# Threshold digits of a mixture-of-experts router moved into an attention loop, counted on GpSimd

## The reference

```python
energy = jnp.einsum('nhqd,nhkd->nhqk', q, k)            # 16 heads of 8, T = 1024
attn = softmax(energy / sqrt(8), axis=3)
out = jnp.einsum('nhql,nhld->nhqd', attn, v)
...
capacity = max(1, int(Sz * CAP_FACTOR / E) + 1)         # 257
scores = softmax(jnp.einsum('bsd,ed->bse', x, router_w), axis=-1)
gate_vals, sel_idx = jax.lax.top_k(swapaxes(scores, 1, 2), capacity)
# tokens = x[b_idx, sel_idx]; two-layer expert with gelu; times gate; scatter-add
```

## Time and profile before

| | us |
|---|---|
| median of 3 runs | 1981.02 (1980.35 to 1981.33) |
| the profiled execution | 1978.19 |
| its span | 1976.4 |
| mean granted TensorE clock of the span | 0.919 of full speed |
| plain attention loop, first to last maximum (L1241) | 1011.4 to 1661.1 |
| its end stretch, to the last division (L1258) | 1661.4 to 1713.0 |

### The profile page before, as it was taken

The page is one execution under the profiler, slowest core; times in us unless marked ns, Lnnn a source line. Parts: engine busy times, 40 slices in busy tenths (PEclk is TensorE's granted clock), DMA queues, the critical chain, the costliest instruction groups (busy, mean ns, idle before and its releaser), DMA issues. The chain is left out here.

```text
span 1976.4 us, 40754 instructions
## 1 busy us (share of the span) xinstructions
PE 1741.5 (88%) x15061; PEld 901.7 (46%) x15061; DVE 1399.7 (71%) x3172; ACT 1151.1 (58%) x2314; POOL 581.1 (29%) x817
## 2 busy tenths in 40 slices
PE   5699999999999968799659999999999999687895
PEld 2356666666666545476312222222232332255563
DVE  6676766767788356542569999999899998656431
ACT  3336666666656632222328898989888887432231
POOL 2312122221122146677440000003310000167774
PEclk9779999999999978879768999999999998689888
DMA  5642744454540053232230000000000000062334
GB/s 162 162 84 50 129 90 78 96 98 72 92 89 12 23 150 60 34 59 36 77 127 9 28 18 18 24 29 18 18 18 24 28 3 23 17 171 38 60 40 84
DMA packets 108005, 120.95 MB, mean 61 GB/s; under 512 B 14360, under 2 KB 72960, under 8 KB 107808
## 3 DMA queue, kind: packets, MB, share of 16 engines
q1 hardware_dynamic: 83616, 100.97, 21.7%
q0 software_dynamic: 24192, 17.38, 6.4%
HBM read 81.71 MB, written 35.65 MB: 59 GB/s over the span
## 5 line engine op out<-in xcount | busy, mean ns | idle before, releaser
L1241 DVE TENSOR_REDUCE mx<-wide 128x2 f32<-128x1024 f32 x512 | 590.8, 1218 | 44.8 <-PE wide L1154 43.4
L1275 ACT ACTIVATE pT<-bank 128x512 f32<-128x512 f32 x1024 | 556.3, 595 | 89.5 <-PE bank L1147 79.1
L903 ACT ACTIVATE pT<-bank 128x512 f32<-128x512 f32 (+3 forms) x768 | 344.0, 490 | 238.8 <-PE bank L757 229.9
L1147 PE MATMUL bank<-q_st,k_st 51*128 51x512 bf16 x1024 | 341.1, 395 | 14.9 <-ACT pT L1275 7.6
L1154 PE MATMUL wide<-k_st,q_st 48*128 48x512 bf16 x1024 | 328.8, 400 | 23.8 <-DVE mx L1241 13.9
L1163 PE MATMUL bank<-pT,vst 128*32 128x256 f32 x4096 | 338.0, 403 | 0.0
L870 DVE TENSOR_REDUCE mx<-wide 128x1 f32<-128x640 f32 (+3 forms) x256 | 256.8, 1021 | 90.6 <-PE wide L772 86.5
L757 PE MATMUL bank<-q_st,k_st 122*128 122x512 f32 (+3 forms) x768 | 297.5, 397 | 6.9 <-ACT pT L903 5.0
L764 PE MATMUL wide<-k_st,q_st 120*128 120x512 f32 (+3 forms) x768 | 270.8, 370 | 20.3 <-PEq L371 11.7
L1860 POOL DMA_INDIRECT acc_rows<-yg,idx x128 | 201.9, 1577 | 102.0 <-DVE yg L2127 66.0
L1147 PEld LDWEIGHTS bank<-q_st,k_st 51*128 51x128 bf16 x1024 | 77.3, 94 | 260.2 <-ACT pT L1275 209.2
(11 more groups left out here) (328 smaller groups left out, 2008.6 us busy)
## 6 DMA issues: line engine op xcount, KB each, us to landing
q_st<-rope_split SPq DMA_DIRECT2D x60, 256.0 KB
k_st<-rope_split SPq DMA_DIRECT2D x60, 256.0 KB
qk_split<-parts SPq DMA_DIRECT2D x8, 1024.0 KB, 6.3
q_st<-qk_split SPq DMA_DIRECT2D x96, 64.0 KB
k_st<-qk_split SPq DMA_DIRECT2D x96, 64.0 KB
qk_parts<-parts SPq DMA_DIRECT2D x8, 768.0 KB, 4.6
xn_rows<-xn SPq DMA_DIRECT2D x8, 512.0 KB, 4.0
w1b<-in_L_ffn_w SPq DMA_DIRECT2D x16, 256.0 KB, 5.2
```

Of the source, the lines that this page charges most:

```text
L903: e.activation(pT[:, u % NPB, q0:HALF], bank[place_of[u]][:, q0:HALF], ACT.Exp, scale=scale).then_inc(s_p, 1)
L1147: e.matmul(bank[place_of[u]][:, :], k_st[at][64 * r:64 * r + KROW, jj, kc * P:(kc + 1) * P], q_st[at][64 * r:64 * r + KROW, jj, J * HALF:( ...
L1241: e.tensor_reduce(mx[G % 2][:, kh, pair:GH:2, c], wide[w % 2][:, :].rearrange("p (r k) -> p r k", r=2), AX.X, ALU.max).then_inc(s_sf, 1)
L1275: e.activation(pT[:, u % NPB, :], bank[place_of[u]][:, :], ACT.Exp, scale=scale).then_inc(s_p, 1)
```

## The change

1. The early steps lie closer. The two norm steps stay in half 18. The other ten stand in halves 19 to 23, two to a half, at begin + 11 and + 14. What is lent is the bank that is idle in that half (`idle_bank`: bank 3 in even halves, 2 in odd ones). GpSimd's multiplications move to t = 304 and 306.
2. Twelve of the 15 digits stand in halves 24 to 29, two to a half. For each, VectorE makes the trials (begin + 3, or + 8), GpSimd counts the hits (in its own program at the same t), TensorE sums the counts into three columns of the idle bank (begin + 7, or + 13), VectorE reads the total (begin + 8, or + 14) and gives the bank back. TensorE waits for the count, and for the bank.
3. GpSimd's count (`pool_digits`) has no accumulator: three comparisons of 128 columns into `hits`, six folds that halve the width, and a last addition into `count`. Behind each of these it waits for its own semaphore.
4. The end stretch keeps `late_step`, and has six steps left of 18: three digits with VectorE's accumulating comparisons, and the three behind the digits.

The diff, cut. Its additions at the end of a t stand in TensorE's loop behind the turn of the maximum (`s_mt`), in VectorE's behind the division of an output (`s_y`), in GpSimd's behind the split (`s_m3`); `digit_read` stands ahead of VectorE's reduce.

```diff
-            lent = bank[3][:, :]
-            routed = Router(buf, 0, lent, lent[:, HALF - 2 * CPH * NE:HALF], results,
-                            (wide[1][:, HALF:2 * HALF], wide[0][:, HALF:2 * HALF]))
+            LENT, COUNTED = range(19, 24), range(24, 30)
+            idle_bank = lambda h: 2 + (h + 1) % 2
+            digits = [(NP * h, first) for h in COUNTED for first in (True, False)]
+            digit_tried = {begin + (3 if first else 8): i for i, (begin, first) in enumerate(digits)}
+            digit_summed = {begin + (7 if first else 13): i for i, (begin, first) in enumerate(digits)}
+            digit_read = {begin + (8 if first else 14): i for i, (begin, first) in enumerate(digits)}
+            lent = [bank[idle_bank(h)][:, :] for h in LENT]
...
-            LENT = range(9, 15)
-            step_at = [2 * NP * s + at for s in LENT for at in (11, 14)]
-            last_of = [2 * NP * s + 14 for s in LENT]
+            step_at = [18 * NP + at for at in (11, 14)] + [NP * h + at for h in LENT for at in (11, 14)]
+            last_of = [NP * h + 14 for h in LENT]
...
-                uses += [(2 * NP * s + 14, 2 * NP * s + 19, 3, ("lent", s)) for s in LENT]
+                uses += [(NP * h + 14, NP * h + 19, idle_bank(h), ("lent", h)) for h in LENT]
+                uses += [(t, t + 2, idle_bank(t // NP), ("digit", i)) for t, i in digit_summed.items()]
...
                                      identb[:, :], start=True, stop=True).then_inc(s_mt, 1)
+                        if t in digit_summed:
+                            bank_free(ahead_of["digit", digit_summed[t]])
+                            next(steps)
...
                          if t in step_at:
                             next(steps)
+                        if t in digit_read:
+                            next(steps)
+                            e.sem_inc(s_lent, 1)
...
                                              rsum[:, :, :, :].broadcast_to([P, CPH, GH, HD]), ALU.mult).then_inc(s_y, 1)
+                        if t in digit_tried:
+                            next(steps)
...
                              next(sums, None)
-                        if t in (19 * NP + 10, 19 * NP + 12):
+                        if t in (19 * NP, 19 * NP + 2):
                             next(normed)
...
                              e.tensor_tensor(part[:, :, 2, :], mxr[:, :, :], part[:, :, 1, :], ALU.subtract).then_inc(s_m3, 1)
+                        if t in digit_tried:
+                            next(counted)
...
+            def pool_digits(self, e):
+                def then(ins):
+                    self.chained += 1
+                    ins.then_inc(self.gp, 1)
+                    e.wait_ge(self.gp, self.chained)
+
+                hits = self.hits
+                for i in range(len(self.sums)):
+                    e.wait_ge(self.inv, i + 2)
+                    for j in range(3):
+                        ins = e.tensor_scalar(hits[:, j, :], self.byrow[:, :], self.trials[:, j:j + 1].bitcast(F32), None, ALU.is_ge)
+                    then(ins)
+                    width = P // 2
+                    while width > 1:
+                        then(e.tensor_tensor(hits[:, :, 0:width], hits[:, :, 0:width], hits[:, :, width:2 * width], ALU.add))
+                        width //= 2
+                    if i:
+                        e.wait_ge(self.tot, PRIME + i)
+                    e.tensor_tensor(self.count[:, :], hits[:, :, 0], hits[:, :, 1], ALU.add).then_inc(self.cnt, 1)
+                    yield
...
                 for i in range(NDIGIT):
-                    if i == 0:
+                    if i < len(self.sums):
+                        if i == 0:
+                            then(e.tensor_copy(self.trials[:, :], digit_units[:, 0, :]))
+                        else:
+                            then(e.scalar_tensor_tensor(self.trials[:, :], digit_units[:, i, :], self.taken[:, 0:1],
+                                                        self.found[:, :].broadcast_to([P, 3]), ALU.bitwise_xor, ALU.bitwise_xor))
+                            mark(e.tensor_tensor(self.found[:, :], self.found[:, :], self.taken[:, :], ALU.bitwise_xor))
+                        e.sem_inc(self.inv, 1)
+                    elif i == 0:
...
-                    e.matmul(self.totals[:, 0:3], same_row[:, :], self.count[:, :], start=True, stop=True).then_inc(self.tot, 1)
+                    e.matmul(self.total_of(i), same_row[:, :], self.count[:, :], start=True, stop=True).then_inc(self.tot, 1)
```

More of the change, by code:

```diff
@@ L1139, in bank_free @@
                             e.wait_ge(s_m, PRIME + n + 1)
+                        elif kind == "digit":
+                            e.wait_ge(s_lent, len(LENT) + n + 1)
                         else:
@@ L1173, in _ @@
                         if t - 3 in step_at:
[L1174 to L1178, removed]
+                            h, at = divmod(t - 3, NP)
+                            if h in LENT and at == 11:
+                                bank_free(ahead_of["lent", h])
                             next(steps)
@@ L1497, in __init__, with logits, total_of @@
                 self.known = sem("gates_known")
-                self.logits = counts[:, 0:CPH * NE].rearrange("p (c e) -> p c e", c=CPH)
+                self.counts = [one[:, HALF - 2 * CPH * NE:HALF] for one in sides] if sides else [counts] * 4
                 self.totals = (late[1] if late else counts)[:, CPH * NE:CPH * NE + 16]
+            def logits(self, q):
+                return self.counts[q][:, 0:CPH * NE].rearrange("p (c e) -> p c e", c=CPH)
+            def total_of(self, i):
+                return self.sums[i] if i < len(self.sums) else self.totals[:, 0:3]
             def xn_of(self, q, c):
@@ L1611, in vector @@
                     e.wait_ge(self.lg, PRIME + q + 1)
-                    then(e.tensor_copy(self.prob[:, q % 2 * CPH:(q % 2 + 1) * CPH, q // 2, :], self.logits))
+                    then(e.tensor_copy(self.prob[:, q % 2 * CPH:(q % 2 + 1) * CPH, q // 2, :], self.logits(q)))
                     yield
@@ L1628, in vector @@
                 e.wait_ge(self.t, PRIME + 1)
-                then(e.tensor_copy(self.byrow[:, :], self.side[:, 0:P]))
+                then(e.tensor_copy(self.byrow[:, :], self.sides[4][:, 0:P]))
                 yield
@@ L1647, in vector @@
                     e.wait_ge(self.tot, PRIME + i + 1)
-                    then(e.tensor_scalar(self.passes[:, :], self.totals[:, 0:3], float(CAP), None, ALU.is_ge, ALU.add,
+                    then(e.tensor_scalar(self.passes[:, :], self.total_of(i), float(CAP), None, ALU.is_ge, ALU.add,
                                          accum_out=self.digit[:, :]))
@@ L1702, in scalar @@
                     e.wait_ge(self.tr, PRIME + q + 1)
-                    e.activation(self.xnT[q % 2][:, :], self.side[:, :], ACT.Copy).then_inc(self.ev, 1)
+                    e.activation(self.xnT[q % 2][:, :], self.sides[q][:, :], ACT.Copy).then_inc(self.ev, 1)
                     yield
@@ L1722, in tensor @@
                     for c in range(CPH):
-                        ins = e.matmul(self.logits[:, c, :], self.xnT[q % 2][:, c * P:(c + 1) * P], rwt[:, :], start=True, stop=True)
+                        ins = e.matmul(self.logits(q)[:, c, :], self.xnT[q % 2][:, c * P:(c + 1) * P], rwt[:, :], start=True, stop=True)
                     ins.then_inc(self.lg, 1)
```

21 lines of the change are left out of this document (13 added, 8 removed).

## The result

The changed kernel takes 2023.20 us (median of 4, 2018.85 to 2028.04), the kernel before in the same comparison 1981.17 us (1980.35 to 1983.75): a ratio of **1.0215, 95% interval 1.0184 to 1.0245**. It is slower by 42 us; 42.6 were forecast. The profiled execution took 2026.51 us.

What follows compares the result with a forecast made beforehand. VectorE (0.9 us slack a half), TensorE and ScalarE, tied by short queues, bound the plain loop. Six halves at +8.1 us, +48.6, less 6 at the end, give +42.6 on 1981.0: 2023.6 us, range 2006 to 2044.

Steps and rivals of the forecast that it cites:

- The wait: TensorE at the product of the maximum (L1229), halves 24 to 29: empty 5.9 us each, split queued behind second count.
- mis-sized term: GpSimd's comparisons in each digit's count: 0.34 us each, three 1.0 us, within a count of 3.7 us.
- a rival with 5 us: GpSimd slower than its rows, 5 us a count: +2 us a half, 2036 us in all; chance 0.08.
- The clock: Behind each wait in halves 24 to 29: slow t's of 2.04 us, 0.8 us lost in each of 2.8, 2.2 us.
- The rival in which the clock holds: Halves 24 to 29 lose only the wait: 6 x 5.9 = 35, less 6, 2010 us; chance 0.08.
- The sum for a half: Each of halves 24 to 29: 6.1 + 2.2 less 0.2, 8.1 us longer; six halves +48.6 us.
- the last term: VectorE's digit work in halves 24 to 29: only the second digit's reading, 0.4 us, counted in the half's sum.
- the rival "not slower": Short wait at the maximum's product, leaving VectorE's 1.2 us a half: 1982 us, or 1979; chance 0.04.
- The end stretch: Last stretch, twelve of 15 digits gone: gain 6 us, between 0 and 9, near 45 us instead of 51.6.
- The first digit's count: GpSimd's first count in halves 24 to 29: done 0.9 us before TensorE wants it, so nobody waits.
- The moved steps: Five routing steps with work, moved to halves 19 to 23: still 2.15 us each, sum of the move 0.
- GpSimd and VectorE: Rival: they contend at the merge of maxima under the first count, 3.5 us over six halves, 2027 us; chance 0.08.

Runs made afterwards that it cites:

- The kernel that holds the clock: Changed kernel plus 48 matmuls whose results are overwritten, on TensorE ahead of its wait for the split in halves 24 to 29; 1987.71 us, ratio 1.0206.
- The split-first kernel: Changed kernel with GpSimd's second count queued behind the split of the maximum; 1956.68 us, ratio 1.004; run again on a third chip 1951.25 us, ratio 1.0013.
- the repeated one: Kernel before and changed kernel, both unchanged, run again on other chips: before 1955.16 us, ratio 1.0012 against itself; changed 1995.76 us, ratio 1.0216.
- the kernel with the steps alone: Kernel before with only the ten early steps moved to halves 19 to 23, all 15 digits left in the end stretch; 1957.68 us, ratio 1.0053.

## Why the prediction was right

**The wait was foreseen with its place and its size.** L1229 waits six times, for L1342, 6.1 us each on TensorE; 5.9 were predicted, and for VectorE's next reduce 5.64 where 5.7 were. Inside it two sizes were off and cancelled. The count is 4.45 us, not 3.7. The folds came out right, 2.32 us for six and 0.20 for the last addition; the comparison was the **mis-sized term**: three took 1.76 us, 0.60 each, where I had 0.34 from a copy of twice the width in 0.40 us. A comparison against a value in memory isn't priced by a copy's row, and I had kept that case for a rival with 5 us. Against that, the count started 0.60 us behind TensorE's arrival (1545.09 to 1545.69), and I had 0.9, plus 0.2 for gaps that were not there: 0.60 + 4.45 + 1.06 = 6.11.

**The clock.** Predicted 2.2 us a half, from the one wait in half 18. The kernel that holds the clock gives 2.2 to 2.3. The slow t's behind the wait are 1.98 us apart, near the 2.04 that I took; I had counted 2.8 of them, and the first half with digits has two, the next one three. The rival in which the clock holds is refuted by 0.82 to 0.88 in the traced halves.

**The sum for a half is 9.0 us, not 8.1** (172.8 us for six against 118.8). By the kernels above it is 5.4 for standing still, 2.2 for the clock and 1.4 for two digits on which nothing waits; I had 5.7, 2.2 and 0.4, less 0.2. So most of the missing 0.9 is in the last term. I had counted only part of the second digit on the path, since VectorE's slack was to hide the rest. The split-first kernel has that term alone, 1.3 to 1.4 us a half, near the 1.2 that I had used in the rival "not slower" and left out of my own sum. VectorE is busy 1.2 us longer in those halves (20.15 us against 18.93), so I take the term for VectorE's; no kernel took its digit instructions away and kept the rest, so this isn't shown.

**The end stretch** was to give 6 us, between 0 and 9, and to take near 45 us. It took 39.2 and gave 12.4 in the profiled pair, beyond my own bound, and 3.5 in the repeated one. I had assumed the first eight t at the low clock of before. ScalarE's timeline of after:

```profile
1725.52 1.57 ACT L1289 ACTIVATE pT<-bank 128x512 f32<-128x512 f32 x3 [1.52 <-PE bank L1155]
...
1740.86 9.03 ACT L1289 ACTIVATE pT<-bank 128x512 f32<-128x512 f32 x18 [0.29 <-PE bank L1155]
1751.15 0.60 ACT L1295 ACTIVATE o_sb<-bank 128x512 f32<-128x512 f32 x1 [1.27 <-PE bank L1171]
```

The clock in that window is 0.96, and the last nine t pass in 9.03 us. With 0.67 before, I take the difference to be mostly clock (no run holds the clock there), and the clock of this stretch is no fixed property: 0.67 and 0.85 in two traces of before, 0.96 and 0.79 in two of after. **So 42.6 was met by luck, because two errors cancelled**: in the traces of the first pair the loop and the end give +55.0 - 12.4 = +42.6, I had +48.6 - 6. With the second pair it is +53.9 - 3.5 = +50.4, and the rest of that kernel was 3.4 us shorter.

**The first digit's count** was to be ready 0.9 us early. With 4.45 us instead of 3.7 that margin is used up. Count, weighing and sum in the second half with digits:

```profile
1569.98 0.64 PE L1171 MATMUL bank<-pT,vst 128*32 128x256 f32 x8
...
1570.26 0.19 POOL L1618 TENSOR_TENSOR count<-hits 128x3 bf16<-128x3 f32 x1
...
1570.60 0.16 PE L1786 MATMUL bank<-count,same_row 128*128 128x3 bf16 x1
```

In all six halves the sum starts 0.34 us behind the start of the count's last instruction, so TensorE takes it as it arrives. That is 0.58 to 0.62 us behind the start of the weighing, and 0.57 to 0.58 for the second digit, whose count is long done: the wait is 0.05 us at most. The rival with a slower GpSimd, 5 us and a wait of 0.4 for the first digit too, didn't happen, but it was close.

**The moved steps** cost nothing in the loop, as predicted: 630.4 us for it in the kernel with the steps alone. The 8 us by which that kernel's median is longer are not explained.

**GpSimd and VectorE** don't get in each other's way here. GpSimd in the first half with digits, and the merge of the maxima, a VectorE instruction on SBUF, under its folds:

```profile
1539.73 2.32 POOL L1614 TENSOR_TENSOR hits<-hits 128x192 f32<-128x192 f32 x6
```

```profile
1540.83 0.18 DVE L1259 TENSOR_TENSOR mxw<-mx 128x16 f32<-128x16 f32 x1
```

In the halves without digits it took 0.17 or 0.18 us, too, and it started as soon behind the reduce ahead of it. The folds of the second count, under which no merge stands, take the same 2.32 us. The Trainium skill (SBUF — State Buffer, "Who interferes with whom") lets the second of two such instructions wait for the first; at 16 columns no trace here shows it.

**What I hadn't in the sum** is that the profiled execution of after is 48.3 us longer than that of before, not 42.6. The part ahead of the loop was 2.5 us shorter, and the second mixture, from VectorE's first reading of an expert's result from a bank to its last, took 8 us more, with the same work on every engine and a lower clock. Windows of before and of after over the same work:

```profile
1748.00:1952.00 204.00, 175.19 (x1279) 121.07 (x1278) 97.24 (x508) 60.19 (x114) 146.25 (x113) 0.92 0.36 61
```

```profile
1788.00:2000.00 212.00, 179.27 (x1281) 124.16 (x1280) 97.62 (x507) 60.22 (x114) 146.37 (x113) 0.89 0.34 59
```

In the repeated pair it is the other way round (192.9 us before, 188.5 after). The 192.9 us of that kernel before:

```profile
1730.40:1923.30 192.90, 171.15 (x1279) 121.02 (x1278) 97.29 (x507) 60.30 (x114) 146.46 (x113) 0.92 0.38 63
```

They come with the same mean clock, 0.92, as the 204.0 of the first chip, so the clock alone doesn't set this length. The change doesn't touch this code, and I take the 8 us for scatter; what makes it was not tried. The medians, which gave 42.0 us, are of four runs each and can't be split into stretches.

## What to carry to other kernels

Before you put new work into a nearly empty engine, look at what stands behind it in that engine's queue, not at how long it takes: here 4.4 us of counting cost 7.6 us a half ahead of a producer, and no wait behind it. A wait of some microseconds on TensorE costs more than its length: here 6.1 us of wait cost the 7.6, of which 2.2 to 2.3 are the clock. And price the work at both places before you move it: where the two prices are nearly alike (11.5 and 8.3 us in the traces, 15.2 and 14.2 by the medians), even the mended version ends level with the kernel before.

## What the runs showed of the hardware

- A GpSimd comparison of 128 float32 columns against a per-partition value in memory takes 0.60 us, while a copy of 256 columns takes 0.39 or 0.40 and a two-input addition of 192 columns 0.59. Six additions that halve the width, from 192 columns to 6, take 2.32 us together.
- With waits of 3.7 us on TensorE the mean clock of the half was 0.81 to 0.87 (0.93 in one of six), with waits of 6.1 us 0.82 to 0.88. With TensorE kept at work until 0.62 us ahead of the awaited product (0.73 on average) the clock stayed at 1.00 in all six halves.
- The same kernel takes 1981 us on one chip and 1949 to 1955 on three others, with plain attention halves of 19.8 us in every trace. Of the 28 us between the two profiled executions of before, 11.3 lie ahead of the plain attention, 6.5 in its end, and 11.1 in the second mixture. The mean clock of the end differs between the two (0.67 and 0.85); that of the mixture is 0.92 in both, and what makes its 11.1 us is open.
